# Attention masks added by VectorE together with the row maximum, instead of by TensorE

## What is computed

```
x = conv_attention(group_norm(x)) + x          # full attention over 256 tokens, 1x1 convolutions
x = x + fire_module(group_norm(x))             # squeeze, 1x1 and 3x3 expand
t = tokens(x)
t = t + attention(layer_norm(t), band mask)    # 8 heads of 16: keys i-63 .. i
t = t + quantized_ffn(layer_norm(t))           # 128 -> 128, binarized weight
t = t + attention(layer_norm(t), causal mask)  # 8 heads of 16: keys 0 .. i
t = t + moe(layer_norm(t))                     # 8 experts 128 -> 512 -> 128, top 2
```

```
P = exp(S + mask - rowmax(S + mask));  out = (P @ V) / rowsum(P)
```

## Time and profile before

| | us |
|---|---|
| median of 3 runs | 235.13 |
| lowest and highest | 234.49, 237.38 |
| the profiled execution | 234.18 |
| its span, from the first to the last instruction | 232.4 |
| PE busy | 222.7 |
| DVE busy | 200.0 |
| ACT busy | 165.2 |
| POOL busy | 84.3 |

### The profile page before, as it was taken

The page is one execution under the profiler, slowest core; times in us unless marked ns, Lnnn a source line. Parts: engine busy times, 40 slices in busy tenths (PEclk is TensorE's granted clock), DMA queues, the critical chain, the costliest instruction groups (busy, mean ns, idle before and its releaser), DMA issues.

```text
span 232.4 us, 4627 instructions
## 1 busy us (share of the span) xinstructions
PE 222.7 (96%) x1493; PEld 172.4 (74%) x1494; DVE 200.0 (86%) x504; ACT 165.2 (71%) x490; POOL 84.3 (36%) x149
## 2 busy tenths in 40 slices
PE   7899898899999999999999999999999999999995
PEld 2697567677776687666866678888888888888885
DVE  4679878986888988999798979999999994999886
ACT  2366355699849986999869999567658766666660
POOL 8201315158965862376515859823000000000000
PEclk9999999999999999999999999999999999999999
DMA  6920000100331201030000324212110005412001
GB/s 176 359 72 4 0 0 0 47 3 5 101 113 19 88 0 42 6 93 1 25 23 1 93 62 129 87 48 45 45 47 0 3 0 159 116 68 70 0 1 45
DMA packets 10999, 12.76 MB, mean 55 GB/s; under 512 B 1232, under 2 KB 7632, under 8 KB 10848
## 3 DMA queue, kind: packets, MB, share of 16 engines
q1 hardware_dynamic: 10544, 12.21, 17.6%
q10 hardware_dynamic: 432, 0.27, 0.4%
HBM read 10.87 MB, written 0.56 MB: 49 GB/s over the span
## 4 chain that ended last, share of the span: by engine, by line
PE 79%; ACT 11%; DVE 4%; DMA 3%; issue 2%; SPq 1%; POOL 0%; ACTq 0%; DVEq 0%
PE bank L996 7%; PE bank L972 7%; PE bank L1084 6%; PE bank L1072 6%; PE bank L1087 6%; PE bank L1085 6%; PE bank L1073 6%; PE bank L1074 6%; ACT early_prob L627 5%; PE bank L1021 5%; PE bank L928 3%; PE bank L939 3%; DMA pk<-packed 3%; PE bank L978 3%; ACT probT L583 2%
## 5 line engine op out<-in xcount | busy, mean ns | idle before, releaser
L657 ACT ACTIVATE hb<-bank,pk 128x512 f32<-128x512 f32 x64 | 43.0, 701 | 21.1 <-PE bank L1074 21.0
L1562 DVE TENSOR_TENSOR hlo<-hb,hhi 128x512 fp32r<-128x512 f32 x64 | 45.1, 727 | 3.2 <-ACT hhi L660 2.1
L627 ACT ACTIVATE prob<-bank,negmax 128x192 f32<-128x192 f32 (+1 forms) x64 | 29.2, 501 | 7.9 <-DVE negmax L1512 7.9
L1512 DVE TENSOR_REDUCE negmax<-bank 128x2 f32<-128x384 f32 (+2 forms) x48 | 29.7, 636 | 3.4 <-PE bank L978 3.0
L473 POOL TENSOR_TENSOR w_lo<-w_raw,w_hi 128x256 fp32r<-128x256 f32 x32 | 25.4, 794 | 2.6
L1084 PE MATMUL bank<-hhi,w_hi 128*128 128x512 f32 (+2 forms) x68 | 25.9, 381 | 0.0
L1087 PE MATMUL bank<-hlo,w_hi 128*128 128x512 f32 (+2 forms) x68 | 25.8, 379 | 0.0
L1085 PE MATMUL bank<-hhi,w_lo 128*128 128x512 f32 (+2 forms) x68 | 25.8, 379 | 0.0
L1072 PE MATMUL bank<-xhi,w_hi 128*128 128x512 f32 x64 | 25.4, 397 | 0.0
L583 ACT ACTIVATE probT<-bank 128x512 f32<-128x512 f32 x38 | 23.1, 646 | 3.3 <-PE bank L996 1.5
L1073 PE MATMUL bank<-xlo,w_hi 128*128 128x512 f32 x64 | 24.9, 390 | 0.0
(11 more groups left out here) (161 smaller groups left out, 510.6 us busy)
## 6 DMA issues: line engine op xcount, KB each, us to landing
w_raw<-w SPq DMA_DIRECT2D x16, 256.0 KB, 3.2
comb_b<-routes SPq DMA_DIRECT2D x16, 256.0 KB, 3.3
pk<-packed SPq DMA_DIRECT2D x1, 1281.0 KB, 8.6
kM<-k_parts SPq DMA_DIRECT2D x32, 32.0 KB, 1.9
pk<-packed SPq DMA_DIRECT2D x1, 560.0 KB, 5.9
xs<-x SPq DMA_DIRECT2D x3, 128.0 KB, 2.7
out<-acc SPq DMA_DIRECT2D x3, 128.0 KB, 1.7
xs<-x ACTq DMA_DIRECT2D x1, 128.0 KB, 2.9
```

The lines of the kernel that those rows point to most:

```text
L627: last = nc.scalar.activation(prob_of(n, u)[:, of], lane[n][u % 2][:, of], ACT.Exp, bias=negmax[n][:, unit_query(u), h:h + 1], accum_out=s ...
L657: nc.scalar.activation(hb[blk % 2][:, j, :], h_bank[j][:, :], ACT.Relu, bias=bias).then_inc(h_ready, 1)
L1512: V.tensor_reduce(negmax[n][:, unit_query(u), heads[0]:heads[-1] + 1], lane[n][u % 2][:, :].rearrange("q (h k) -> q h k", h=len(heads))[:, ...
L1562: V.tensor_tensor(hlo[blk % 2][:, j, :], hb[blk % 2][:, j, :], hhi[blk % 2][:, j, :].bitcast(F32), ALU.subtract).then_inc(hlo_ready, 1)
```

## The change

The mask matmul is removed. The masks are kept as 32-bit floats in SBUF. For each head of a unit DVE runs a `tensor_tensor_reduce`: it adds the mask to the scores in PSUM, multiplies by -1, writes the result to a new SBUF tile `masked` (two units for each lane), and in the same instruction takes the minimum over the row, which is minus the maximum. ACT's exponentials read `masked` with scale -1. Since nothing reads the score bank after DVE, PE waits for `max_ready` of unit u-2 in place of `exp_done`, and so do the projections of the next pass, the second layer norm's transposes, the transposes of the routes and the first hidden product. DVE gets a wait in return: `masked` may be rewritten only once the exponentials of unit u-2 (or those of the pass before) are done. The tile that keeps PE's clock up in the first part is now a view of `masked`.

```diff
-    aq=256, ak=256, av=128, ao=128, ident_bf=64, band0=64, band1=128, fw=128, fb=256, mean=128,
-    cq=256, ck=256, cv=128, co=128, causal0=64, causal1=128, headmask=8, halves=2, router=8,
+    aq=256, ak=256, av=128, ao=128, band0=128, band1=256, fw=128, fb=256, mean=128,
+    cq=256, ck=256, cv=128, co=128, causal1=256, headmask=8, halves=2, router=8,
...
+        masked = each("masked", [128, 2, 512], n=2, scope=attention_memory)
+        idle_work = masked[0][:, 0, 0:256].bitcast(BF16)
...
                     last = nc.scalar.activation(
-                        prob_of(n, u)[:, of], lane[n][u % 2][:, of], ACT.Exp,
-                        bias=negmax[n][:, unit_query(u), h:h + 1], accum_out=sums[n][:, unit_query(u), row(h) // HD:row(h) // HD + 1])
+                        prob_of(n, u)[:, of], masked[n % 2][:, u % 2, of], ACT.Exp,
+                        bias=negmax[n][:, unit_query(u), h:h + 1], scale=-1.0, accum_out=sums[n][:, unit_query(u), row(h) // HD:row(h) // HD + 1])
...
@@ scores, and in the same way turn (j == 2), project_keys, project_queries, turn_routes, hidden @@
                 if u >= 2:
 
-                    pe.wait_ge(exp_done[n], a * UNITS + u - 1)
+                    pe.wait_ge(max_ready[n], a * UNITS + u - 1)
...
                 for part in (q_hi, q_lo):
-                    mm(dst[:, :, keys], part[n % 2][:, g, i * 128:(i + 1) * 128],
-                       kM[n % 2][:, heads[0]:heads[-1] + 1, keys],
-                       start=(part is q_hi), stop=False, skip_group_check=True)
-                seen = slice(128, T) if (a, i) == (1, 1) else keys
-                dst = dst[:, :, seen]
-                mask = A_MASK[a][i][:, seen].unsqueeze(1).to_broadcast(list(dst.shape))
-                mm(dst, ident_bf, mask, start=False, stop=True, skip_group_check=True).then_inc(s_full[n], 1)
+                    last = mm(dst[:, :, keys], part[n % 2][:, g, i * 128:(i + 1) * 128],
+                              kM[n % 2][:, heads[0]:heads[-1] + 1, keys],
+                              start=(part is q_hi), stop=(part is q_lo), skip_group_check=True)
+                last.then_inc(s_full[n], 1)
...
             def largest(a, n, u):
                 dve.wait_ge(s_full[n], a * UNITS + u + 1)
-                heads = unit_heads(n, u)
-                V.tensor_reduce(negmax[n][:, unit_query(u), heads[0]:heads[-1] + 1],
-                                lane[n][u % 2][:, :].rearrange("q (h k) -> q h k", h=len(heads))[:, :, unit_keys(a, u)],
-                                AX.X, ALU.max, negate=True).then_inc(max_ready[n], 1)
+                if u >= 2:
+
+                    dve.wait_ge(exp_done[n], a * UNITS + u - 1)
+                elif passed(a, n):
+                    b, m = earlier(a, n)
+                    dve.wait_ge(exp_done[m], b * UNITS + UNITS - 1 + u)
+                i, width, keys = unit_query(u), unit_width(u), unit_keys(a, u)
+                for at, h in enumerate(unit_heads(n, u)):
+                    of = slice(at * width + keys.start, at * width + keys.stop)
+                    scored = lane[n][u % 2][:, of]
+                    last = V.tensor_tensor_reduce(
+                        out=masked[n % 2][:, u % 2, of], in0=scored, in1=A_MASK[a][i][:, keys], scale=-1.0, scalar=LARGEST,
+                        op0=ALU.add, op1=ALU.min, accum_out=negmax[n][:, i, h:h + 1])
+                last.then_inc(max_ready[n], 1)
```

More of the change, by code:

```diff
@@ L33 @@
 NEG = -1e30
+LARGEST = 3e38
 ROUND = 1.5 * 2.0 ** 23
@@ L94, in build @@
         ident = const("ident")
-        ident_bf = const("ident_bf").bitcast(BF16)
         neghalf = sb("neghalf", [128, B])
-        idle_work = sb("idle_work", [128, 512], BF16)
         bq_scaled = sb("bq_scaled", [128, 1])
@@ L241, in build @@
         A_WQ, A_WK, A_WV, A_WO = ([const(f"{layer}{n}") for layer in "ac"] for n in "qkvo")
-        A_MASK = [[const(f"{kind}{i}").bitcast(BF16) for i in range(TT)] for kind in ("band", "causal")]
+        A_MASK = [[const("band0"), const("band1")], [const("causal1", 128, 256), const("causal1")]]
         IS_LOW, SIGNED_SCALE = const("halves", 0, 1), const("halves", 1, 2)
@@ L898, in turn @@
                     b, m = earlier(1, n)
-                    pe.wait_ge(exp_done[m], b * UNITS + UNITS - 1)
+                    pe.wait_ge(max_ready[m], b * UNITS + UNITS - 1)
                 for i in range(TT):
@@ L925, in project_keys @@
                     b, m = earlier(a, n)
-                    pe.wait_ge(exp_done[m], (b + 1) * UNITS)
+                    pe.wait_ge(max_ready[m], (b + 1) * UNITS)
                 for g in range(2):
@@ L1045, in turn_routes @@
                 if h == 0:
-                    pe.wait_ge(exp_done[3], 2 * UNITS)
+                    pe.wait_ge(max_ready[3], 2 * UNITS)
                 for i in range(NT // 2):
@@ L1068, in hidden @@
                     else:
-                        pe.wait_ge(exp_done[2 + j // 2], 2 * UNITS - 1 + j % 2)
+                        pe.wait_ge(max_ready[2 + j // 2], 2 * UNITS - 1 + j % 2)
                     chunk = slice(j * 128, (j + 1) * 128)
@@ L1684, in tokens @@
                     dve.wait_ge(dve_step, done[n])
-            V.memset(idle_work[:, :], 0.0).then_inc(idle_work_ready, 1)
+            V.memset(idle_work, 0.0).then_inc(idle_work_ready, 1)
             first_stats(0, 0, xs)
@@ L1972 @@
     ki = np.arange(256)[None, :]
-    def bf16_pairs(v):
-        bits = v.astype(f32).view(np.uint32)
-        return ((bits + 0x7FFF + ((bits >> 16) & 1)) >> 16).astype(np.uint16).view(f32)
     def mask(valid):
-        return bf16_pairs(np.where(valid, 0.0, NEG))
+        return np.where(valid, 0.0, NEG).astype(f32)
     band = [(ki <= qi + 128 * i) & (ki > qi + 128 * i - 64) for i in range(2)]
-    causal = [ki <= qi + 128 * i for i in range(2)]
+    causal = ki <= qi + 128
     ch = np.arange(128)
@@ L1992 @@
         ao=paired_rows(a["L2_attn_Wo"].T),
-        ident_bf=bf16_pairs(np.eye(128)), band0=mask(band[0][:, 0:128]), band1=mask(band[1]),
+        band0=mask(band[0][:, 0:128]), band1=mask(band[1]),
         fw=a["L2_ffn_weight"], fb=np.tile(a["L2_ffn_bias"][None, :], (128, 2)),
@@ L1997 @@
         cv=a["L3_attn_W_V"].reshape(128, 128).T, co=paired_rows(a["L3_attn_W_O"].T),
-        causal0=mask(causal[0][:, 0:128]), causal1=mask(causal[1]),
+        causal1=mask(causal),
         headmask=(ch[:, None] // HP == np.arange(HEADS)[None, :] % HG).astype(f32),
```

## The result

The changed kernel takes 238.09 us (median of 4 runs, 237.26 to 240.1) against 234.90 for the kernel before in the same comparison: a ratio of 1.0132, with a 95% interval of 1.0079 to 1.0184. So it is slower, by 1.3%, which is 3.2 us. The prediction had said 246, 11 us more, and had given a change of under 2% one chance in nine.

What follows compares the result with a forecast made beforehand. DVE was to become the bound of the attention passes: 82.1 us of work + 16.3 added + 7.8 idle = 106.2 against 95.4, +10.8 us, giving a median of 246 us; forecast range 239.5 to 258, 8 in 10 range 237 to 262.

Steps and rivals of the forecast that it cites:

- the pair's price: DVE, attention passes: each fused instruction plus accumulator read costs 0.15 us above its columns (bounds 0.13 and 0.305).
- 16.3 us more DVE work: DVE, attention passes: 128 pairs at 0.15 us, less 2.9 us for the 48 old reduces; bounds 13.7 and 36.1.
- rival 1: Faster: DVE's accumulator read hides behind the next stream, 0.06 us a pair, 228.6 us in all; chance 0.05.
- the test named at the end of the prediction: DVE pieces' start-to-start distance: 0.29 us forecast for 128 columns; under 0.24 us the prediction is wrong.
- Rival 2: No difference: 0.10 us a pair on DVE, 4 us idle left in the passes, 235.7 us; chance 0.11.
- stays below what DVE will need, so I don't add it: ACT's exponentials reading SBUF: 0.03 us each, 4 us over four passes, ACT from 84.7 to 89 us, not added.
- The rule of the sum: Attention passes: DVE's work plus 7.8 us of remaining idle time sets their length, 106.2 us against 95.4.
- PE's mask matmuls: Removing them takes 8.6 us of PE work, gained nowhere since PE waits for DVE and ACT.
- DVE's waits for scores: Attention passes: the 3.0 us that DVE waits for scores go once PE has slack.
- The new wait of DVE: DVE's wait for `exp_done` of unit u-2 ends earlier than the old wait did; cost none.
- The constants: Packed constants grow by 192 columns, 98 KB; the transfer's first reader is not on the chain, so they cost nothing.
- rival 3: Much slower: DVE's pair does not overlap (266 us) or the fused instruction streams at half rate (270 us); chance 0.14.

Runs made afterwards that it cites:

- one reduce a head: The kernel before with one reduce for each head in place of one for each unit, without masks or accumulators: 236.87 us, ratio 1.0091.
- the kernel without pairs: The kernel before with exponentials reading a constant SBUF tile, PE waiting on `max_ready`, and no mask matmuls; DVE's single reduces kept: 236.33 us, ratio 1.0023.
- the kernel with casts: The changed kernel with a one-element copy on DVE ahead of each fused instruction: 243.45 us, ratio 1.0353 to the kernel before.

## Why the prediction was wrong

**The term that failed: the pair's price.** "I take 0.06 + 0.09 = 0.15 us" measured 0.08, and "16.3 us more DVE work" measured 6.4 us. With 0.08 the prediction's own formula gives 128 x 0.08 - 2.9 = 7.3. The error was to take the read's distance from ACT, where a read adds 0.09 to 0.10 us, and to require DVE's small steps to add up as in the index search. On DVE the read is shown as 81 ns long and costs hardly anything, since the next piece starts with it: a pair costs 0.013 us more than a reduce without a read. The text had that case as rival 1 but gave it 0.05. It is the test named at the end of the prediction, under 0.24 us for 128 columns, that told this. The rival's own time, 228.6, was wrong too: it let DVE's idle time fall to 2 us, and 98.95 - 88.55 = 10.4 us of it stayed. ACT's longer steps are not needed for that: one reduce a head, with ACT as before, left 10.9. Rival 2, no difference, had a change of under 2%, and that is what was measured, but it went another way: 0.10 us a pair, 4 us of idle time and 235.7 us. That it came nearest of the rivals is luck.

**The step that failed: ACT "stays below what DVE will need, so I don't add it".** Its size, 0.03 us each and 4 us in all, was nearly right (0.04 and 4.6). Left out, it is the largest single loss: alone it costs 3.0 us. The prediction's first part had read from the chain that the inner stretches go by ACT; a lengthening there was bound to show unless DVE passed ACT in each stretch. The sum compared totals over the passes, and took the larger. With the right DVE figure the totals would have been 88.5 and 89.4, and the rule, 88.5 + 7.8 = 96.3, gives +0.9 us against the +3.1 measured. So two errors partly cancelled: 9.9 us too much DVE work, and ACT's 3 us left out.

**The rule of the sum.** "DVE becomes the bound of the passes" gives nearly the right length at 94.9 us of DVE work (102.7 by the rule, 103.6 measured) and not at 88.5 (96.3 by the rule, 98.95 measured). Two engines share the path by turns: from the kernel without pairs to the changed one, 5.1 us of DVE work cost 1.4 us of passes; from there to the kernel with casts, 6.4 us more cost 4.65. Even there not all of DVE's work shows, and ACT keeps 14% of the chain.

**What held.** PE's mask matmuls gain little: 0.8 to 1.4 us of 8.6 (the prediction had none). DVE's waits for scores go (3.0 to 0.6). The new wait of DVE does not appear among its waits. The constants cost nothing. The experts keep their time. The instruction streams at the full rate with one source in PSUM and one in SBUF, and rival 3 is out. The Trainium skill, Vector Engine (DVE) Microarchitecture Reference, section Points that are easy to get wrong, names a halved rate for two SBUF sources only; that is not contradicted here, and no run has two. The 120 cycles (0.125 us) of the Trainium skill, VectorE: DVE Perf Modes, section on the TRN2 errata, were further from the 0.08 us measured than the rows' 0.06.

**What stays open.** Why seven tenths of ACT's addition, made first, and only a quarter of DVE's, made last, show in the time is argued from the chain, not tried stretch by stretch; nor was the order of the steps turned round, which would say how much of it is the order. Why a read of SBUF adds 0.04 us on ACT is not shown, only that it does.

## What to carry to other kernels

For an engine that the chain shows in a stretch, add a cost even when the engine's total stays below another's; compare the engines by stretch, not over the whole. Moving an operand from PSUM to SBUF to release a bank is not free for its reader: here, by the profiles, the release gave 0.5 to 0.8 us (1.5 by the ratios) and the SBUF source took 3.0. Splitting one instruction in several has a price of its own, whatever the pieces do: 4.6 of DVE's 6.4 us. And the price of a step on one engine says little of the same step on another: an accumulator read costs ACT 0.09 us and DVE next to nothing.

## What was not expected of the hardware

- On DVE the read of an accumulator lies behind the next instruction: pieces of 128, 192 and 256 columns start 0.21, 0.28 and 0.34 us apart, while the read's row says 81 ns. Reduces without a read start 0.20, 0.27 and 0.33 us apart. On ACT it is paid, 0.09 to 0.10 us.
- The same DVE instruction costs more when it writes to PSUM: 0.25 us in place of 0.21 from start to start for 128 columns, and its read 139 ns in place of 81.
- An exponential on ACT costs 0.04 us more when it reads SBUF than when it reads PSUM, at 128, 192 and 256 columns alike.
- A one-element cast of 148 ns between pieces adds only 0.06 us to their distance.
- In one kernel a wait of PE of 1.57 us was followed by 6 us at a granted clock of 0.50; in another a wait of 1.60 us at the same place was not (PE busy for 4.4 of the 6 us around it, clock 1.00).
